# Attention in half heads: query columns in halves, row maxima 28 pairs ahead

## The chip, the cores and the metric

One Trainium2 chip, and of it one core. The metric is the time of one execution in microseconds on the device (us). The program is one launch: a mixture-of-experts layer, an attention layer, and a second mixture-of-experts layer.

## What is computed

Two sequences of 2048 tokens with 128 channels go through three residual blocks. The middle one is attention with 16 heads of 8 channels, so with both sequences there are 32 heads of 2048 queries by 2048 keys:

```python
q = _apply_rope(_rms_norm(x @ wq.T), rope_cos, rope_sin) / math.sqrt(HEAD_DIM)
k = _apply_rope(_rms_norm(x @ wk.T), rope_cos, rope_sin)
scores = jnp.einsum('bqhd,bkhd->bhqk', q, k)
attn = jax.nn.softmax(scores.astype(jnp.float32), axis=-1)
out = jnp.einsum('bhqk,bkhd->bqhd', attn, v).reshape(b, s, hidden)
return out @ wo.T
...
x = x + 0.5 * ffn(layernorm(x))
x = x + attention(layernorm(x))
x = x + 0.5 * ffn(layernorm(x))
```

The softmax needs the maximum of each query's row of scores before any exponential of that row can be taken.

## The kernel before

**Phases.** Loading, the first expert phase (`e1`), projections with rotation (`qk`), `attention_phase`, and the second expert phase (`e3`). Between phases all engines meet. What is changed lies in `attention_phase`, lines 1014 to 1326, and in the class `Late` behind it.

**Two passes over the scores.** In the first, TensorE multiplies 128 queries with 1024 keys into two banks of PSUM (`maxima`, line 1213, two matmuls of 512 columns: a *pair*), and VectorE reduces the pair to one maximum for each query (line 1301). A head has 32 pairs. The banks of two pairs alternate (`MRING = 2`), so TensorE writes a pair when VectorE has done the last but one. When all pairs of a head are reduced, VectorE takes the negative maximum (line 1315, *find*), GpSimd splits it into three bf16 parts (lines 1095 to 1101), TensorE turns them into rows (line 1226, *turn*), ScalarE copies those (line 1181), and a DMA places them beside the rows of `q_head` (line 1128). In the second pass TensorE multiplies 128 keys with 512 queries (`scores`, line 1231), and since the negative maxima are rows of the operand, the product has them subtracted. ScalarE takes the exponential out of PSUM (line 1168, *exp*). Four matmuls beside each other (`weigh`, line 1241) weigh the values with two such blocks, 1024 queries, and add up in one bank (`O`). Three banks hold scores (`SRING = 3`): the matmul for block n waits for exp n-3.

**The order.** Each engine runs a list written out by hand. I call one *step* what weighs 1024 queries with 128 keys: two score matmuls, two exps, four weighing matmuls, and, beside the scores and on other rows of the array, one pair for the maxima of a later head. A head has 32 steps. On TensorE a step is: scores, half a pair, scores, half a pair, and then the weighing of the step two before. The maxima run ahead in this way: 46 pairs stand before the first scores, and from then on (`LAG = 9`) the pairs of the head after next follow those of the next head. The turn of a head stands at its step 25 of 32, and takes one of the three score banks in its turn.

**Sums.** When a head's last step is weighed, ScalarE copies bank `O` out (`keep_sums`, line 1175), and TensorE's first weighing of the next head waits for that copy (line 1239). On ScalarE the copy stands behind the first two steps' exps of the next head. SyncE then stores the sums (line 1134) and loads `q_head` and `k_head` of the third head from there in 12 DMAs.

**Late work.** While the last steps run, and VectorE has no more maxima, the first sequence's attention output is divided, projected, added, normalized and routed (`tail_pe`, `tail_act`, `tail_dve`, numbered slots of which one stands behind each step; the highest, 37 to 40, turn the routing weights, line 1572, and VectorE copies them, line 1577). `store_comb` writes those weights to HBM, and `e3` begins by loading them from there (`e_cw`, line 733).

Of the kernel before, what the change touches and what calls it, by code (L numbers as in the profile page):

```python
# [19 lines left out]
P = 128  # L20
# [22 lines left out]
PROBS = 4  # L43
# [9 lines left out]
MR = 3  # L53
# [960 lines left out]
def attention_phase(nc, sem, kept, ps, v, identb, q, k, vals, q_rows, k_rows, qk_loaded, qk_stored,  # L1014
# [9 lines left out]
    CHUNKS = SEQ // BLK  # L1024
    STEPS = KT * CHUNKS
    PAIRS_OF_HEAD = STEPS // 2
    ENTRIES = STEPS + 1
    AHEAD, LAG = 2, 9
    TURNS = BH - AHEAD
# [4 lines left out]
    TURN_MAXIMA = LAG + 3  # L1034
    TAIL_FROM = (BH - 2) * KT + LAG + 1

    def tail(h, g, half):

        return 2 * (h * KT + g - TAIL_FROM) + half

    assert TURNS % BUFS == 0 and BUFS * ENTRIES % SRING == 0 and PAIRS_OF_HEAD % MRING == 0
# [12 lines left out]
    def turned_at(h):  # L1054

        return 0 if isinstance(h, int) and h == 0 else 1 + (h - 1) * ENTRIES + 4 * (TURN_MAXIMA + 1)

    def entry(h, g, c, last=False):

        return 1 + h * ENTRIES + g * CHUNKS + c + (1 if g > TURN_MAXIMA and not last else 0)  # L1060

    def bank(i, g, c, last=False):

        return (1 + i * ENTRIES + g * CHUNKS + c + (1 if g > TURN_MAXIMA and not last else 0)) % SRING

    def turned_bank(i):

        return (1 + (i - 1) * ENTRIES + 4 * (TURN_MAXIMA + 1)) % SRING

    with ExitStack() as tmp:  # L1070
        mx = [kept(f"mx{i}", [P, KT, 2]) for i in range(BUFS)]
        neg = [kept(f"neg{i}", [P, KT]) for i in range(BUFS)]
        res = kept("res", [P, KT])
        zero = kept("zero", [P, KT])
        mparts = [kept(f"mparts{i}", [P, MR, KT], BF16) for i in range(BUFS)]
        mrows = kept("mrows", [MR * KT, P], BF16)
# [7 lines left out]
        def _(pool):  # L1084
            def place(h, i):
                head = v[:].rearrange("p b h t d -> p (b h) t d")[:, h, :, :]
                pool.tensor_copy(vals[i][:, :, 0:HD], head).then_inc(values_placed, 1)  # L1087

            def split(h, i):

                at = h * VSTEPS
                pool.wait_ge(max_found, h + 1)
                if not (isinstance(h, int) and h < BUFS):
                    pool.wait_ge(scored, turned_at(h - BUFS) + 1)
# [8 lines left out]
            def replace(h, i):  # L1103
                pool.wait_ge(weighed, (h + 1) * KT + PRIME)
                place(h + BUFS, i)

            pool.memset(zero[:], 0.0).then_inc(max_zeroed, 1)
            for i in range(BUFS):
                place(i, i)
            pool.wait_ge(max_zeroed, 1)  # L1110
            for h in range(2 * BUFS):
                split(h, h % BUFS)
                if h:
                    replace(h - 1, (h - 1) % BUFS)
            for it in range(2, BH // BUFS - 1):
                for i in range(BUFS):
                    split(it * BUFS + i, i)
                    replace(it * BUFS + i - 1, (i - 1) % BUFS)
            for h in range((BH // BUFS - 1) * BUFS, BH):
                split(h, h % BUFS)  # L1120
                if h - 1 + BUFS < BH:
                    replace(h - 1, (h - 1) % BUFS)

        @block.sync
        def _(sp):
            def place_maxima(h, i):
                sp.wait_ge(exped, turned_at(h) + 1)
                sp.dma_start(q[i][MROW:MROW + MR, :], mrows[:]).then_inc(max_placed, 16)
# [7 lines left out]
            def turn(h, i):  # L1136
                place_maxima(h + 1, (i + 1) % BUFS)
                sp.wait_ge(weighed, (h + 1) * KT + PRIME)
                load_head(sp, q[i], k[i], q_rows[h + BUFS], k_rows[h + BUFS], qk_loaded[i])
                store_sums(h)  # L1140

            prime(sp, sums_stored)
            for h in range(1, BUFS):
                load_head(sp, q[h], k[h], q_rows[h], k_rows[h], qk_loaded[h])
            for i in range(len(qk_stored)):
                sp.wait_ge(qk_stored[i], 16 * 2 * len(range(i, NB, len(qk_stored))))
            place_maxima(0, 0)
            for it in range(0, BH // BUFS - 1):
                for i in range(BUFS):
                    turn(it * BUFS + i, i)  # L1150
            for h in range((BH // BUFS - 1) * BUFS, BH):
                if h < BH - BUFS:
                    turn(h, h % BUFS)
                else:
                    if h < BH - 1:
                        place_maxima(h + 1, (h + 1) % BUFS)
                    store_sums(h)
                if h == BH - 3:
                    late.load_sums(sp, 0)
                if h == BH - 2:  # L1160
                    late.store_comb(sp, 0)

        @block.scalar
        def _(act):
            def exps(h, i, g, last=False):
                for c in range(CHUNKS):
                    act.wait_ge(scored, entry(h, g, c, last) + 1)
                    act.activation(prob[:, g % PROBS, c, :], ps[:, S + bank(i, g, c, last), :], ACT.Exp).then_inc(exped, 1)  # L1168
                    if c % 2:
                        late.tail_act(act, tail(h, g, c // 2), M)  # L1170

            def keep_sums(h):
                act.wait_ge(weighed, (h + 1) * KT + PRIME)
# [3 lines left out]
            def keep_maxima(h, bank_at):  # L1177
                act.wait_ge(scored, turned_at(h) + 1)
                if not (isinstance(h, int) and h == 0):
                    act.wait_ge(max_placed, 16 * h)  # L1180
                act.activation(mrows[:], ps[0:MR * KT, S + bank_at, 0:P], ACT.Copy).then_inc(exped, 1)

            def turn(h, i, last=False):
                for g in range(1, KT):
                    if not (isinstance(h, int) and h == 0 and g < PROBS):

                        act.wait_ge(weighed, h * KT + max(g - PROBS, -1) + 1 + PRIME)
                    exps(h, i, g, last)
                    if g == TURN_MAXIMA and not last:
                        keep_maxima(h + 1, turned_bank(i + 1))  # L1190
# [6 lines left out]
            keep_maxima(0, 0)  # L1197
            exps(0, 0, 0)
            for it in range(0, TURNS // BUFS):
                for i in range(BUFS):  # L1200
                    turn(it * BUFS + i, i)
            turn(BH - 2, (BH - 2) % BUFS)
            turn(BH - 1, (BH - 1) % BUFS, last=True)

        @block.tensor
        def _(pe):
            def maxima(h, i, j):

                n, c = h * PAIRS_OF_HEAD + j // 2, j % CHUNKS
                if j % 2 == 0 and not (isinstance(n, int) and n < MRING):  # L1210
                    pe.wait_ge(max_reduced, n - MRING + 1)
                at = M + 2 * (j // 2 % MRING) + j % 2
                one = pe.matmul(ps[:, at, :], q[i][HALF:HALF + KR, (j // CHUNKS) * P:(j // CHUNKS + 1) * P],  # L1213
                                k[i][HALF:HALF + KR, c * BLK:(c + 1) * BLK], start=True, stop=True)
                if j % 2:
                    one.then_inc(max_scored, 1)

            def free(n):

                if not (isinstance(n, int) and n < SRING):  # L1220
                    pe.wait_ge(exped, n - SRING + 1)

            def turn_maxima(h, i, bank_at):
                free(turned_at(h))
                pe.wait_ge(max_split, (h + 1) * VSTEPS)
                pe.matmul(ps[0:MR * KT, S + bank_at, 0:P], mparts[i][:].rearrange("p a t -> p (a t)"), identb[:],
                          start=True, stop=True).then_inc(scored, 1)

            def scores(h, i, g, c, last=False):
                free(entry(h, g, c, last))  # L1230
                pe.matmul(ps[:, S + bank(i, g, c, last), :], k[i][0:KS, g * P:(g + 1) * P],  # L1231
                          q[i][0:KS, c * BLK:(c + 1) * BLK], start=True, stop=True).then_inc(scored, 1)

            def weigh(h, i, g, half, last=False):

                pe.wait_ge(exped, entry(h, g, 2 * half + 1, last) + 1)
# [3 lines left out]
                for j in range(4):  # L1240
                    done_one = pe.matmul(ps[32 * j:32 * j + 32, O, half * HALF_BLK:(half + 1) * HALF_BLK], vals[i][:, g, :],  # L1241
# [621 lines left out]
```

## Time and profile before

| | |
|---|---|
| median of 3 runs | 1897.98 us |
| lowest and highest | 1893.78 and 1899.74 us |
| span of the profiled execution | 1896.1 us |
| instructions in it | 37685 |
| TensorE busy | 1781.2 us, 94% |
| VectorE busy | 1620.7 us, 85% |
| ScalarE busy | 1459.6 us, 77% |
| GpSimd busy | 344.2 us, 18% |
| attention phase, first maxima to the first load of `e3` | 386.54 to 1638.65 us |

The profiler's span runs from the first to the last instruction. It is the profiled execution's own time as far as the page has one, and it stands 1.9 us below the median of the runs. PE is TensorE, DVE VectorE, ACT ScalarE, POOL GpSimd, SP SyncE, and PEld is TensorE's load of weights. The ends of matmuls are modelled and overlap, so a busy PE can still have time to give; the distance from the start of a matmul to the start of the same matmul one step later says more. An instruction's row names what ended the idle time before it.

### The profile page before, as it was taken

To read this page: it belongs to the slowest core of one execution; us is meant where nothing else is said; L and a number is where in the kernel's file an instruction comes from. 1 tells how busy PE (TensorE), PEld (TensorE's weight loads), DVE (VectorE), ACT (ScalarE), POOL (GpSimd) and SP (SyncE) were. 2 spreads that over 40 slices of the span, in tenths; PEclk is the share of its full clock that TensorE was granted. 3 is DMA by queue.
4 is the path that set the end of the run, shared out by engine and by line. 5 is a ranking of instruction groups with operands and counts; after the bars stand their busy time and mean duration, and the time that the engine had idled before them with its cause. 6 is when DMAs were issued, how large, how long until landed. Compare 5 with 4: busy or idle time off the path is not lost. (4 is left out here: it accounts for less than half of the span.)

```text
span 1896.1 us, 37685 instructions
## 1 busy us (share of the span) xinstructions
PE 1781.2 (94%) x14923; PEld 750.2 (40%) x14923; DVE 1620.7 (85%) x1950; ACT 1459.6 (77%) x2715; POOL 344.2 (18%) x416
## 2 busy tenths in 40 slices
PE   5699998879999999999999999999999999899998
PEld 3488776702222222222222222222222223377786
DVE  6466775689999999999999999999999993386765
ACT  2356564606999999999999999999999996546455
POOL 4266551300000000000000000000000000145565
PEclk9799997857999999999999999999999998999999
DMA  4453330220010010000001001000000010444463
GB/s 117 88 128 127 103 110 1 93 91 2 25 33 20 20 36 22 20 31 27 20 25 33 20 20 37 21 20 31 26 20 26 33 28 3 85 109 109 102 144 78
DMA packets 66309, 98.81 MB, mean 52 GB/s; under 512 B 11995, under 2 KB 33312, under 8 KB 66116
## 3 DMA queue, kind: packets, MB, share of 16 engines
q1 hardware_dynamic: 61974, 94.32, 18.4%
q10 hardware_dynamic: 4160, 2.10, 0.4%
q8 instruction: 117, 1.92, 0.4%
q14 instruction: 58, 0.48, 0.1%
HBM read 84.94 MB, written 11.04 MB: 51 GB/s over the span
## 5 line engine op out<-in xcount | busy, mean ns | idle before, releaser
L1301 DVE TENSOR_REDUCE at_mx<-ps 128x1 f32<-128x1024 f32 x1024 | 1166.1, 1216 | 9.8 <-PE ps L1213 7.7
L1168 ACT ACTIVATE at_prob<-ps 128x512 f32<-128x512 f32 x2048 | 1098.2, 596 | 77.0 <-PE ps L1231 31.8
L1241 PE MATMUL ps<-at_prob,vals 128*32 128x256 f32 x8192 | 656.9, 392 | 13.3 <-ACT at_sums L1175 13.3
L1213 PE MATMUL ps<-k_head,q_head 48*128 48x512 bf16 x2048 | 638.8, 392 | 14.3 <-PEq L800 7.5
L1231 PE MATMUL ps<-q_head,k_head 51*128 51x512 bf16 x1924 | 584.5, 383 | 2.8 <-ACT at_prob L1168 2.8
L1241 PEld LDWEIGHTS ps<-at_prob,vals 128*32 128x32 f32 x8192 | 162.4, 108 | 429.5 <-ACT at_prob L1168 409.0
L688 POOL TENSOR_TENSOR e_part<-e_silu,e_cw 128x512 f32<-128x512 f32 (+1 forms) x208 | 268.1, 1289 | 311.5 <-ACT e_silu L659 124.3
L700 DVE TENSOR_TENSOR ps<-e_part,ps 128x512 f32<-128x512 f32 (+1 forms) x208 | 144.5, 695 | 157.6 <-POOL e_part L688 157.1
L1231 PEld LDWEIGHTS ps<-q_head,k_head 51*128 51x128 bf16 x1924 | 117.5, 93 | 404.1 <-ACT at_prob L1168 385.3
L659 ACT ACTIVATE e_silu<-ps 128x512 f32<-128x512 f32 (+1 forms) x208 | 124.2, 597 | 143.8 <-PE ps L615 141.9
L1095 POOL TENSOR_TENSOR at_mparts<-at_neg,at_zero 128x16 bf16<-128x16 f32 x32 | 7.0, 220 | 796.5 <-DVE at_neg L1315 796.5
L1213 PEld LDWEIGHTS ps<-k_head,q_head 48*128 48x128 bf16 x2048 | 119.8, 94 | 55.2 <-DVE at_mx L1301 44.8
L666 ACT ACTIVATE q_head<-ps 128x512 fp32r<-128x512 f32 (+1 forms) x156 | 93.1, 597 | 44.8 <-DVE ps L700 34.2
L615 PE MATMUL ps<-xnT_hi,wgate_hi 128*128 128x512 f32 x208 | 88.6, 426 | 20.0 <-ACT e_silu L659 13.7
L706 DVE TENSOR_TENSOR q_head<-ps,q_head 128x512 fp32r<-128x512 f32 (+1 forms) x156 | 106.6, 684 | 0.4
L633 PE MATMUL ps<-q_head,wdown_hi 128*128 128x512 f32 (+1 forms) x312 | 98.1, 395 | 2.4 <-DVE q_head L706 2.4
L615 PE MATMUL ps<-xnT_lo,wgate_hi 128*128 128x512 f32 x208 | 82.6, 397 | 0.0
L615 PE MATMUL ps<-xnT_hi,wgate_lo 128*128 128x512 f32 x208 | 82.2, 395 | 0.0
L623 PE MATMUL ps<-xnT_hi,wup_hi 128*128 128x512 f32 x192 | 76.1, 396 | 0.0
L623 PE MATMUL ps<-xnT_lo,wup_hi 128*128 128x512 f32 x192 | 75.9, 395 | 0.0
L623 PE MATMUL ps<-xnT_hi,wup_lo 128*128 128x512 f32 x192 | 75.8, 395 | 0.0
L1087 POOL COPY vals<-v 128x128 f32<-128x128 f32 x32 | 9.1, 290 | 332.6 <-PE ps L1241 332.6
(258 smaller groups left out, 1294.2 us busy)
## 6 DMA issues: line engine op xcount, KB each, us to landing
e_cw<-comb_rows SPq DMA_DIRECT2D x80, 256.0 KB, 3.3
e_cw<-comb_rows SPq DMA_DIRECT2D x32, 224.0 KB, 3.1
e_cw<-comb_rows SPq DMA_DIRECT2D x32, 192.0 KB, 3.3
q_head<-q_rows SPq DMA_DIRECT2D x64, 96.0 KB
k_head<-k_rows SPq DMA_DIRECT2D x64, 96.0 KB
e_cw<-comb_rows SPq DMA_DIRECT2D x32, 160.0 KB, 2.9
e_cw<-comb_rows SPq DMA_DIRECT2D x48, 96.0 KB, 2.8
e_cw<-comb_rows SPq DMA_DIRECT2D x32, 128.0 KB, 3.1
```

Of the source, the lines that this page charges most:

```text
L615: last = pe.matmul(ps[:, gate_bank(n), :], wgate[wp][:, cols], xnT[xp][:, tokens], start=(m == 0), stop=(m == len(PASSES) - 1))
L623: last = pe.matmul(ps[:, UP + n % UPS, :], wup[wp][:, cols], xnT[xp][:, tokens], start=(m == 0), stop=(m == len(PASSES) - 1))
L633: last = pe.matmul(ps[:, Y, :], wdown[wp][0:rows[c], c, :], hidden[hp][n % HIDDENS][0:rows[c], :], start=(c == 0 and m == 0), stop=(c == C ...
L659: act.activation(silu[0:r, n % 2, :], ps[0:r, gate_bank(n), :], ACT.Silu).then_inc(silued, 1)
L688: pool.tensor_tensor(part[0:r, n % 2, :], silu[0:r, n % 2, :], cw[0:r, n % CW, :], ALU.mult).then_inc(weighted, 1)
L700: dve.tensor_tensor(ps[0:rows[c], UP + n % UPS, :], part[0:rows[c], n % 2, :], up, ALU.mult).then_inc(product, 1)
L706: dve.tensor_tensor(hidden[LO][n % HIDDENS][0:r, :], ps[0:r, UP + n % UPS, :], hidden[HI][n % HIDDENS][0:r, :].bitcast(F32), ALU.subtract) ...
L1168: act.activation(prob[:, g % PROBS, c, :], ps[:, S + bank(i, g, c, last), :], ACT.Exp).then_inc(exped, 1)
L1213: one = pe.matmul(ps[:, at, :], q[i][HALF:HALF + KR, (j // CHUNKS) * P:(j // CHUNKS + 1) * P], k[i][HALF:HALF + KR, c * BLK:(c + 1) * BLK] ...
L1231: pe.matmul(ps[:, S + bank(i, g, c, last), :], k[i][0:KS, g * P:(g + 1) * P], q[i][0:KS, c * BLK:(c + 1) * BLK], start=True, stop=True).th ...
L1241: done_one = pe.matmul(ps[32 * j:32 * j + 32, O, half * HALF_BLK:(half + 1) * HALF_BLK], vals[i][:, g, :], prob[:, g % PROBS, 2 * half + j ...
L1301: dve.tensor_reduce(mx[i][:, j // 2, j % 2:j % 2 + 1], ps[:, at:at + 2, :].rearrange("p a t -> p (a t)"), AX.X, ALU.max).then_inc(max_redu ...
```

## The change

A *unit* is now half a head: 16 key tiles by 1024 queries, 16 steps and 16 pairs. There are 64 units. The maxima of a unit cover only its 1024 queries, and find, split, turn, copy and placing DMA are done for each unit, on half the columns: 64 times instead of 32. The pairs run `LEAD = 28` steps ahead of the scores, all along, so 28 pairs stand before the first scores. A step is what it was: the same two score matmuls, two exps, a pair, and the weighing of the step two before (`WEIGH_AFTER = 2`). The exps of the two halves of a key tile, which were neighbours, are now 16 steps apart, and the probabilities have 8 slots of one step instead of 4 slots of two, in the same memory.

Around that, four things move. The turn stands behind step 9 of each unit, and behind the step's weighing instead of ahead of its second half. `keep_sums` stands behind the exps of step 2 of the next head. SyncE's order in a head becomes: store sums, place maxima, load, place maxima; and at the end `store_comb` stands behind the last store of sums. The late work begins at step 997 of 1024, where it began at step 980, and its slots from 29 on (of 41) stand behind the attention's last step.

The core of the diff:

```diff
-PROBS = 4
+PROBS = 8
...
-    PAIRS_OF_HEAD = STEPS // 2
-    ENTRIES = STEPS + 1
-    AHEAD, LAG = 2, 9
-    TURNS = BH - AHEAD
+    UNITS = 2 * BH
+    CHUNKS = 2
+    TILES = SEQ // P // 2
+    PAIRS_OF_UNIT = 2 * TILES
+    STEPS = UNITS * KT
+    ENTRIES = KT * CHUNKS + 1
+    LEAD = PAIRS_OF_UNIT + 12
+    TURN = 9
+    WEIGH_AFTER = 2
...
-    TURN_MAXIMA = LAG + 3
-    TAIL_FROM = (BH - 2) * KT + LAG + 1
...
+    TAIL_FROM = STEPS - LEAD + 1
...
         @block.sync
...
+            for h in range(BH):
+                if h >= 1:
+                    store_sums(h - 1)
+                place_maxima(2 * h + 1)
+                if h >= 1 and h - 1 + BUFS < BH:
+                    sp.wait_ge(weighed, head_done(h - 1))
+                    load(h - 1 + BUFS)
+                if h < BH - 1:
+                    place_maxima(2 * h + 2)
                 if h == BH - 2:
-                    late.store_comb(sp, 0)
+                    late.load_sums(sp, 0)
+            store_sums(BH - 1)
+            late.store_comb(sp, 0)
...
         @block.scalar
...
+            def exps(t):
+                if t >= PROBS:
+                    act.wait_ge(weighed, t - PROBS + 1 + PRIME)
                 for c in range(CHUNKS):
...
-                if not last:
-                    act.wait_ge(weighed, (h + 1) * KT - PROBS + 1 + PRIME)
-                    exps(h + 1, i + 1, 0)
-                keep_sums(h)
...
+            for t in range(STEPS):
+                u, g = divmod(t, KT)
+                exps(t)
+                if g == TURN and u < UNITS - 1:
+                    keep_maxima(u + 1)
+                late.tail_act(act, t - TAIL_FROM, M)
+                if t >= 2 * KT and t % (2 * KT) == WEIGH_AFTER:
+                    keep_sums(t // (2 * KT) - 1)
+            keep_sums(BH - 1)
+            for t in range(STEPS, TAIL_FROM + late.TAIL):
+                late.tail_act(act, t - TAIL_FROM, M)
...
         @block.tensor
...
+            for r in range(LEAD):
+                for one in range(2):
+                    maxima(r, one)
+                if r == PAIRS_OF_UNIT + 4:
+                    turn_maxima(0)
+            for t in range(STEPS + WEIGH_AFTER):
+                u, g = divmod(t, KT)
+                for c in range(CHUNKS):
+                    if t < STEPS:
+                        scores(t, c)
+                    if t + LEAD < STEPS:
+                        maxima(t + LEAD, c)
+                if t >= WEIGH_AFTER:
+                    weigh(t - WEIGH_AFTER)
+                if g == TURN and u < UNITS - 1:
+                    turn_maxima(u + 1)
+                late.tail_pe(pe, t - TAIL_FROM, M)
...
         @block.vector
...
+            for r in range(STEPS):
+                reduce(r)
+                if r >= PAIRS_OF_UNIT and r % PAIRS_OF_UNIT == 1:
+                    find(r // PAIRS_OF_UNIT - 1)
+            find(UNITS - 1)
```

Ahead of the first scores on TensorE (the names: `k_head` by `q_head` is a matmul for maxima, `identb` a turn, `q_head` by `k_head` scores) stood, before:

```order
L1213 MATMUL ps<-k_head0,q_head0 128x512 x64
L1213 MATMUL ps<-k_head1,q_head1 128x512 x13
L1226 MATMUL ps<-identb,at_mparts0 48x128
L1213 MATMUL ps<-k_head1,q_head1 128x512 x15
L1231 MATMUL ps<-q_head0,k_head0 128x512 x5
```

and now:

```order
L1194 MATMUL ps<-k_head0,q_head0 128x512 x42
L1208 MATMUL ps<-identb,at_mparts0 24x128
L1194 MATMUL ps<-k_head0,q_head0 128x512 x14
L1218 MATMUL ps<-q_head0,k_head0 128x512
L1194 MATMUL ps<-k_head0,q_head0 128x512
L1218 MATMUL ps<-q_head0,k_head0 128x512
```

The 92 matmuls for maxima before the first scores have become 56, and all of them are of the first head.

On ScalarE, from the first exps to the third head (`at_prob` is an exp, `at_mrows` the copy of turned maxima, `at_sums` the copy of the sums), stood, before:

```order
L1168 ACTIVATE at_prob<-ps 128x512 x52
L1181 ACTIVATE at_mrows<-ps 48x128
L1168 ACTIVATE at_prob<-ps 128x512 x16
L1175 ACTIVATE at_sums<-ps 128x512
L1168 ACTIVATE at_prob<-ps 128x512 x48
L1181 ACTIVATE at_mrows<-ps 48x128
L1168 ACTIVATE at_prob<-ps 128x512 x16
L1175 ACTIVATE at_sums<-ps 128x512
```

and now:

```order
L1155 ACTIVATE at_prob<-ps 128x512 x20
L1167 ACTIVATE at_mrows<-ps 24x128
L1155 ACTIVATE at_prob<-ps 128x512 x32
L1167 ACTIVATE at_mrows<-ps 24x128
L1155 ACTIVATE at_prob<-ps 128x512 x18
L1160 ACTIVATE at_sums<-ps 128x512
L1155 ACTIVATE at_prob<-ps 128x512 x14
L1167 ACTIVATE at_mrows<-ps 24x128
L1155 ACTIVATE at_prob<-ps 128x512 x32
```

A head has 64 exps. The first copy of sums stood behind 68 of them, 4 of the next head, and stands behind 70, 6 of the next head; the copies of maxima stand twice in a head.

At the end of the phase SyncE had, behind its loads of the late work (`at_o`), before:

```order
L1128 DMA q_head<-at_mrows 3x16x128
L1134 DMA sum_rows<-at_sums 18x1x256 x4
L1582 DMA comb_rows<-v 9x2048
L1134 DMA sum_rows<-at_sums 18x1x256 x4
L1070 UNCONDITIONAL_BRANCH
```

and now:

```order
L1121 DMA sum_rows<-at_sums 18x1x256 x4
L1115 DMA q_head<-at_mrows 3x8x128
L1121 DMA sum_rows<-at_sums 18x1x256 x4
L1536 DMA comb_rows<-v 9x2048
L1066 UNCONDITIONAL_BRANCH
```

The store of the routing weights (`comb_rows`) has moved behind the last sums and is the last DMA of the phase.

## Rows read from the trace of the kernel before

**Rows 1.** The page: engines' busy us; a group's busy us, mean ns.

```profile
PE 1781.2 (94%) x14923; PEld 750.2 (40%) x14923; DVE 1620.7 (85%) x1950; ACT 1459.6 (77%) x2715; POOL 344.2 (18%) x416
...
L1301 DVE TENSOR_REDUCE at_mx<-ps 128x1 f32<-128x1024 f32 x1024 | 1166.1, 1216 | 9.8 <-PE ps L1213 7.7
```

**Rows 2.** Stretches: us, then busy time of PE, PEld, DVE, ACT, POOL, and PEclk.

```profile
386.00:440.00 54.00, 46.56 (x93) 6.36 (x95) 52.02 (x46) 1.55 (x2) 1.68 (x8) 0.50 0.11 41
439.79:446.38 6.59, 6.30 (x32) 1.25 (x34) 4.73 (x4) 4.13 (x8) 0.00 (x0) 0.50 0.01 4
478.00:1535.00 1057.00, 1044.61 (x11167) 269.00 (x11165) 1054.98 (x958) 1009.83 (x1915) 33.78 (x145) 1.00 0.08 26
1589.84:1603.49 13.65, 13.65 (x67) 5.03 (x59) 4.12 (x11) 6.55 (x13) 0.00 (x0) 0.50 0.00 1
```

**Rows 3.** Instructions in order: start, us, engine; first maxima, first scores.

```profile
386.54 1.86 PE L1213 MATMUL ps<-k_head,q_head 48*128 48x512 bf16 x4 [7.45 <-PEq L800]
...
439.79 0.60 PE L1231 MATMUL ps<-q_head,k_head 51*128 51x512 bf16 x1
```

**Rows 4.** Instructions in order: steps in the middle of a head.

```profile
999.36 6.87 DVE L1301 TENSOR_REDUCE at_mx<-ps 128x1 f32<-128x1024 f32 x6
...
1000.74 0.39 PE L1231 MATMUL ps<-q_head,k_head 51*128 51x512 bf16 x1
...
1001.28 0.64 PE L1241 MATMUL ps<-at_prob,vals 128*32 128x256 f32 x8
...
1004.60 0.64 PE L1241 MATMUL ps<-at_prob,vals 128*32 128x256 f32 x8
```

**Rows 5.** Instructions in order: the boundary between two heads; the next copy of sums.

```profile
989.60 1.08 ACT L1168 ACTIVATE at_prob<-ps 128x512 f32<-128x512 f32 x2
989.71 0.64 PE L1241 MATMUL ps<-at_prob,vals 128*32 128x256 f32 x8
...
990.57 0.60 ACT L1175 ACTIVATE at_sums<-ps 128x512 f32<-128x512 f32 x1
...
991.32 0.64 PE L1241 MATMUL ps<-at_prob,vals 128*32 128x256 f32 x8 [0.43 <-ACT at_sums L1175]
...
1027.02 0.60 ACT L1175 ACTIVATE at_sums<-ps 128x512 f32<-128x512 f32 x1
```

**Rows 6.** Instructions in order: a turn on PE, and ACT behind it.

```profile
1017.09 0.24 PE L1226 MATMUL ps<-identb,at_mparts 128*48 128x128 bf16 x1
1017.26 0.64 PE L1241 MATMUL ps<-at_prob,vals 128*32 128x256 f32 x8
1017.83 0.39 PE L1231 MATMUL ps<-q_head,k_head 51*128 51x512 bf16 x1
...
1018.32 1.09 ACT L1168 ACTIVATE at_prob<-ps 128x512 f32<-128x512 f32 x2
```

**Rows 7.** The tile of the sums: ns min/median/max of one, first and last start.

```profile
L1175 ACT ACTIVATE at_sums<-ps x32: 597/605/605, 480.2 to 1634.1; 128x512 f32<-128x512 f32 x32
```

**Rows 8.** Instructions in order: from the last maxima to the first load of `e3`.

```profile
1557.62 0.60 PE L1231 MATMUL ps<-q_head,k_head 51*128 51x512 bf16 x2
...
1589.16 0.39 PE L1231 MATMUL ps<-q_head,k_head 51*128 51x512 bf16 x1 [2.47 <-ACT at_prob L1168]
...
1622.27 0.26 DVE L1565 RECIPROCAL at_comb<-at_ex 128x16 f32<-128x16 f32 x1
...
1629.70 0.68 DVE L1577 COPY v<-ps 9x512 f32<-9x512 f32 x1 [0.96 <-PE ps L1572]
...
1638.65 2.22 SPq L733 DMA_DIRECT2D e_cw<-comb_rows  x5
```

**Rows 9.** The chain that ended last: start, us; the same store for the second sequence.

```profile
1775.80 2.41 DMA comb_rows<-v
```

**Rows 10.** Instructions in order: two steps at the lower clock, first head.

```profile
444.07 0.60 PE L1231 MATMUL ps<-q_head,k_head 51*128 51x512 bf16 x1
...
446.05 0.53 PE L1231 MATMUL ps<-q_head,k_head 51*128 51x512 bf16 x1
```

More of the change, by code:

```diff
@@ L1142, in _ @@
             prime(sp, sums_stored)
             for h in range(1, BUFS):
-                load_head(sp, q[h], k[h], q_rows[h], k_rows[h], qk_loaded[h])
+                load(h)
             for i in range(len(qk_stored)):
                 sp.wait_ge(qk_stored[i], 16 * 2 * len(range(i, NB, len(qk_stored))))
[L1147 to L1158, printed above, removed]
+            place_maxima(0)
@@ L1196, in _, with keep_maxima @@
-            prime(act, sums_kept)
[L1197 to L1203, printed above, removed]
+            def keep_maxima(u):
+                n = turned_at(u)
+                act.wait_ge(scored, n + 1)
+                if u:
+                    act.wait_ge(max_placed, 16 * u)
+                act.activation(mrows[:], ps[0:MR * TILES, S + n % SRING, 0:P], ACT.Copy).then_inc(exped, 1)
@@ L1205, in _, with maxima @@
         @block.tensor
         def _(pe):
[L1207 to L1216, printed above, removed]
+            def maxima(r, one):
+                u, j = divmod(r, PAIRS_OF_UNIT)
+                h, half = divmod(u, 2)
+                if one == 0 and r % (2 * PAIRS_OF_UNIT) == 0:
+                    pe.wait_ge(qk_loaded[h % BUFS], 16 * LOAD_DMAS * (h // BUFS + 1))
+                if one == 0 and r >= MRING:
+                    pe.wait_ge(max_reduced, r - MRING + 1)
+                tile, c = half * TILES + j // 2, 2 * (j % 2) + one
+                made = pe.matmul(ps[:, M + 2 * (r % MRING) + one, :], q[h % BUFS][HALF:HALF + KR, tile * P:(tile + 1) * P],
+                                 k[h % BUFS][HALF:HALF + KR, c * BLK:(c + 1) * BLK], start=True, stop=True)
+                if one:
+                    made.then_inc(max_scored, 1)
@@ L1218, in free @@
             def free(n):
-                if not (isinstance(n, int) and n < SRING):
+                if n >= SRING:
                     pe.wait_ge(exped, n - SRING + 1)
[L1223 to L1226, printed above, removed]
-                          start=True, stop=True).then_inc(scored, 1)
[L1229 to L1232, printed above, removed]
@@ L1234, in weigh, with turn_maxima, scores @@
-            def weigh(h, i, g, half, last=False):
-                pe.wait_ge(exped, entry(h, g, 2 * half + 1, last) + 1)
+            def turn_maxima(u):
+                n = turned_at(u)
+                free(n)
+                pe.wait_ge(max_split, (u + 1) * VSTEPS)
+                pe.matmul(ps[0:MR * TILES, S + n % SRING, 0:P], mparts[u % BUFS][:].rearrange("p a t -> p (a t)"), identb[:],
+                          start=True, stop=True).then_inc(scored, 1)
+            def scores(t, c):
+                u, g = divmod(t, KT)
+                h, half = divmod(u, 2)
+                n, at = entry(t, c), (2 * half + c) * BLK
+                if g == 0 and c == 0:
+                    pe.wait_ge(max_placed, 16 * (u + 1))
+                free(n)
+                pe.matmul(ps[:, S + n % SRING, :], k[h % BUFS][0:KS, g * P:(g + 1) * P],
+                          q[h % BUFS][0:KS, at:at + BLK], start=True, stop=True).then_inc(scored, 1)
@@ L1273, in pe_next @@
-            def pe_next(h, nxt, c, i):
-                free(entry(h + 1, 0, c))
-                pe.matmul(ps[:, S + bank(i + 1, 0, c), :], k[nxt][0:KS, 0:P],
-                          q[nxt][0:KS, c * BLK:(c + 1) * BLK], start=True, stop=True).then_inc(scored, 1)
-            prime(pe, weighed)
-            for h in range(AHEAD):
-                pe.wait_ge(qk_loaded[h], 16 * LOAD_DMAS)
-                for j in range(STEPS if h == 0 else (KT - LAG) * CHUNKS):
-                    maxima(h, h, j)
-                    if h == 1 and j == 3 * CHUNKS:
-                        turn_maxima(0, 0, 0)
```

192 lines of the change are left out of this document (65 added, 127 removed).

## The prediction, made before the changed kernel ran

> **What bounds the kernel now.** I read the page's busy times first, then stretches, then single steps. Over the whole span TensorE is 94% busy and VectorE 85% [rows 1], which is a mean over stages; attention alone takes 1252 us of the 1896 [rows 3, 8], and there the stretch of 29 heads says more: of 1057 us VectorE is busy 1054.98, TensorE 1044.61, ScalarE 1009.83 [rows 2]. Three engines are close together, so I take each engine's own pace. VectorE: six reductions in a row take 6.87 us [rows 4]; less the last one's own 1.216 [rows 1], five distances are 5.65, so 1.131 a pair. TensorE, where it waits for nobody: from one weighing to the third after it 3.32 us, so 1.107 a step [rows 4]. A head is 36.45 us from one copy of sums to the next [rows 5]. VectorE's 32 pairs are 36.2 of that, and the find fills most of the rest. VectorE sets the pace, and TensorE has 32 x 1.107 = 35.4 of its own, plus what interrupts it: 0.5 at the boundary, where the first weighing of a head stands 1.61 us behind the last of the one before instead of 1.107, released by the copy of sums [rows 5], and some 0.2 at a turn [rows 6]. So TensorE needs 36.1 of 36.45. It is 0.3 us a head from being the bound, and that margin is what I watch in this change.
>
> **The change part by part.**
>
> *Fewer pairs ahead.* Before the first scores VectorE is the one that is busy (52.02 of 54 us), at TensorE's lower clock [rows 2], and the first scores start with the 46th pair: 439.79 - 386.54 = 53.25 us for 45 pairs, 1.183 each [rows 3]. Now they start with the 28th: 27 x 1.183 = 31.9. **Gain 21.3 us.** The unit's turn stands 7 pairs ahead of that, 8 us, for a copy and a small DMA; before it had 7 as well.
>
> *A step.* The matmuls, exps and pairs of a step are the same in number and size, and so is the distance from exp to weighing. Each pair of exps now has a second wait (slots of one step); before every other one had it. The wait is long satisfied, and from the start of a pair of exps to what follows on ScalarE are 0.97 us [rows 5], so 0.13 a step lies free under TensorE's 1.107. I take nothing; only what a second wait costs beyond 0.13 would add to each of 1024 steps.
>
> *The boundary.* This is the large term. `keep_sums` stands behind the exps of the third step of a head, not the second, while TensorE's first weighing still stands directly behind the third step's scores and waits for that copy. Counted from the start of the third step's first score: ScalarE's pair of exps starts 0.49 us after it (1017.83 to 1018.32) [rows 6]; the copy of sums follows 0.97 after the pair's start, and the weighing is released 0.75 after the copy's start (989.60, 990.57, 991.32) [rows 5]. So the weighing starts at 2.21, where it would start at 0.54 (1000.74 to 1001.28) [rows 4]. TensorE waits **1.67 us at each boundary instead of 0.50**. Behind the waiting weighing stand, in TensorE's order, the next step's scores and maxima, so VectorE, which has one pair ready, runs dry too, about 1.4 us. Bounds: no less than 0.5 if the copy got in between the exps, which its place in the list excludes; no more than 1.8, if the second wait uses up those 0.13.
>
> *The turn.* Twice a head, for half the columns. The matmul delays what stands behind it 0.17 us (1017.09 to 1017.26) [rows 6]. The turn takes one score bank, so the second score of the next step waits for an exp that ends about 1.58 us after the turning step's start (0.49, a distance of 0.49, and 0.60) while it would start at 1.51; with its release that is 0.12 more. So 0.29 each, bounds 0.17 and 0.40. The chain ahead of it (find, four short GpSimd operations) has two pairs' time, 2.26 us, and the DMA behind it has 6 steps, as before; I take nothing for either. The second find adds less than 0.1 us on VectorE, which is no longer the bound.
>
> *Loads and stores.* On SyncE 12 loads now stand between the two placings of a head, 13 steps ahead of the second; at 0.44 an issue (five in 2.22) [rows 8] that is 5 us, at twice as much 11. The loaded head is wanted 25 steps later, 28 us. I take nothing.
>
> *The attention loop, summed.* From the first score to the first step without maxima TensorE has 997 steps: 997 x 1.107 = 1103.7. Boundaries in it: 31 x 1.67 = 51.8. Turns: 62 x 0.29 = 18.0. The start at the lower clock: the first copy of sums is at 480.2 [rows 7], 40.4 us after the first score, where 33 steps, a turn and 1.46 to the copy make 38.2; the start costs 2.2, now as before. Sum 1175.7. VectorE's need in the same loop is 997 x 1.131 + 62 x 0.09 = 1133, so TensorE is the bound by a wide margin: 37.7 us a head. Before, the loop was 1557.62 - 439.79 = 1117.8 [rows 3, 8] for 980 steps. **Loss 57.9 us**, of which 19 are the 17 more steps with maxima that the shorter lead shifts here.
>
> *The late work.* Before, `e3`'s first load was issued 81.0 us after the first step without maxima (1557.62 to 1638.65), with attention's own end and its stores in between; the routing weights were ready at 64.9 (1622.27 and 0.26) and copied by 72.8 (1629.70 and 0.68) [rows 8]. VectorE's chain up to the weights I leave at 64.9: its slots up to 28 still lie beside attention steps. Then the four turns and copies stand alone: between 4 x 0.68 + 0.6 = 3.3 and, with TensorE at the lower clock after waiting, 5; I take 4.7. The store is now on the path: 2.4 [rows 9] and its issue 0.3. So 72.3 or 72.5 instead of 81.0. **Gain 8.5 us**, bounds 5 and 11. `e3` itself is untouched.
>
> Sum against the profiled span: 1896.1 - 21.3 + 57.9 - 8.5 = 1924.2. The median of the runs is 1.9 above the span, so **1926 us**. The bounds of the boundary, turn and late work give 1915 to 1938.
>
> **The rivals.**
>
> *The clock falls too.* In the late work TensorE stood idle 2.47 us [rows 8], and right behind that its granted clock was 0.50, the 1.2 GHz level, for 13.65 us; in the 29 heads, with 0.43 us of idling at each boundary, it stayed at 1.00 [rows 2, 5]. The new idling at each boundary is 1.6 us, between the two. A step at the lower clock is 1.98 us [rows 10] for 1.107. At the start the clock came back 6.6 us after the first scores [rows 2]; a fall as long costs 6.6 x (1 - 1.107/1.98) = 2.9 us. At half of the boundaries that is 45 us: 1971; at a few of them, 1935 to 1950. For it: the idling comes at every head. Against: two thirds of the row's 2.47 us, with dense work on both sides. By the Trainium skill ("TensorE: Matmul & The Clock Gate", section "HAM oscillation — how this bites in real kernels") a wait that recurs in every turn of a loop can throttle the clock anew in every turn; no run here shows that yet, and the 0.50 behind the 2.47 us agrees that one wait can do it. Chance 0.13.
>
> *The boundary is hidden, no change.* If the weighing waited 0.5 us as before (the copy not really behind those exps, or TensorE's later matmuls passing it), TensorE's need is 35.4 + 0.5 + 0.6 = 36.5 and VectorE's 36.4: 36.6 a head, 31 x 1.1 = 34 us less than forecast, 1892 to 1900. Against it: in the rows the engines keep their written order [rows 5]. Chance 0.11.
>
> *Faster.* If TensorE's interruptions overlap with VectorE's backlog so that heads stay at 36.45, the loop is 997/980 of before, plus 19, and the sum is 1896.1 - 21.3 + 19 - 8.5 + 1.9 = 1887. It decides at a TensorE need of 36.4 a head; I find 37.7. Chance 0.06.
>
> **How the numbers follow.** Forecast 0.70, clock 0.13, no change 0.11, faster 0.06. About 0.3% (6 us) can be told from no change: faster 0.07, same 0.12, slower 0.81. The forecast's own range is 1915 to 1938; it reaches on to part of the clock's case and a little way towards no change: 1908 to 1952.
>
> **What would show it.** Right: first scores 31.9 us after the first maxima; a row of weighing at each of 31 boundaries with the copy of sums as its releaser and some 1.6 us of idling (about 50 us in all); copies of sums 37.7 us apart; VectorE idle over 1 us a head; granted clock 1.00 in the heads; `e3`'s first load about 72 us after the last maxima. Wrong: copies 36.5 apart (no or little stall), a granted clock under 1.00 in the middle stretch (the clock), turns that wait for the split, or late work that takes 80 us as before.

## The result, and the profile after

The changed kernel takes **1936.45 us** (median of four runs, 1934.51 to 1952.33), the kernel before 1896.57 (1893.78 to 1899.74): a ratio of 1.0231, 95% interval 1.0193 to 1.0270. The profiled execution's span is 1933.9 us against 1896.1, so 37.8 us more.

The page's busy times of the changed kernel, and three of its costliest groups (busy us, mean ns of one, then idle time of the engine just before and what ended it; L1265 reduces, L1230 weighs, L1155 are the exps), which answer to [rows 1]:

```profile
PE 1775.8 (92%) x14955; PEld 752.7 (39%) x14955; DVE 1625.4 (84%) x1982; ACT 1476.6 (76%) x2747; POOL 365.3 (19%) x544
...
L1265 DVE TENSOR_REDUCE at_mx<-ps 128x1 f32<-128x1024 f32 x1024 | 1170.9, 1216 | 57.3 <-PE ps L1194 56.9
L1155 ACT ACTIVATE at_prob<-ps 128x512 f32<-128x512 f32 x2048 | 1110.2, 595 | 115.2 <-PE ps L1218 94.4
L1230 PE MATMUL ps<-at_prob,vals 128*32 128x256 f32 x8192 | 663.5, 396 | 49.5 <-ACT at_sums L1160 49.5
```

A reduction lasts 1216 ns as before. What is new is waiting: VectorE idles 57.3 us ahead of its reductions, where it was 9.8 [rows 1], and TensorE 49.5 us ahead of weighings, all of it ended by the copy of sums.

Stretches of the changed kernel (us, then busy time of PE, PEld, DVE, ACT, POOL, PEclk, DMA share, GB/s): the maxima alone, the start of the loop, some 30 heads, and one stretch inside these.

```profile
379.50:411.56 32.06, 27.81 (x56) 3.74 (x56) 30.68 (x28) 1.55 (x2) 1.61 (x8) 0.50 0.19 68
411.56:417.70 6.14, 5.71 (x26) 0.94 (x26) 5.82 (x5) 3.36 (x6) 0.00 (x0) 0.50 0.00 0
454.00:1591.00 1137.00, 1084.65 (x11484) 281.91 (x11484) 1087.34 (x1013) 1050.68 (x1995) 54.64 (x269) 0.99 0.07 24
494.35:497.76 3.41, 3.41 (x24) 0.47 (x16) 2.40 (x2) 1.96 (x5) 0.00 (x0) 0.50 0.11 22
```

In the long stretch no engine is full any more: VectorE, full within 2 us of 1057 before [rows 2], is idle 50 us of 1137. And the granted clock, 1.00 in the heads before, is 0.99, with stretches at 0.50.

The boundary in order (start, us, engine, line; in brackets the engine's idle time and what ended it), first one at which the clock fell, then the next, at which it didn't, with the copy after it:

```profile
492.30 0.61 ACT L1160 ACTIVATE at_sums<-ps 128x512 f32<-128x512 f32 x1
...
493.05 0.64 PE L1230 MATMUL ps<-at_prob,vals 128*32 128x256 f32 x8 [1.60 <-ACT at_sums L1160]
...
494.30 1.22 DVE L1265 TENSOR_REDUCE at_mx<-ps 128x1 f32<-128x1024 f32 x1 [1.30 <-PE ps L1194]
495.04 0.60 PE L1218 MATMUL ps<-q_head,k_head 51*128 51x512 bf16 x1
...
497.02 0.60 PE L1218 MATMUL ps<-q_head,k_head 51*128 51x512 bf16 x1
...
529.60 0.64 PE L1230 MATMUL ps<-at_prob,vals 128*32 128x256 f32 x8
...
531.62 0.61 ACT L1160 ACTIVATE at_sums<-ps 128x512 f32<-128x512 f32 x1
...
532.38 0.64 PE L1230 MATMUL ps<-at_prob,vals 128*32 128x256 f32 x8 [1.60 <-ACT at_sums L1160]
...
569.42 0.60 ACT L1160 ACTIVATE at_sums<-ps 128x512 f32<-128x512 f32 x1
```

The weighing that stood 1.61 us behind the last one [rows 5] stands 532.38 - 529.60 = 2.78 behind it, so it waits 2.78 - 1.107 = 1.67 us. From copy to copy it is 37.80 us (531.62 to 569.42), before 36.45 [rows 5]. After the first of the two boundaries it is 39.32 (492.30 to 531.62): there one step (495.04 to 497.02) takes the 1.98 us of the lower clock [rows 10]. Of the 31 boundaries 8 are like that one, and 23 like the second.

A turn in order, ahead of the next weighing; then the find of the same head's second unit (L1273) between weighings, with the second turn ahead of the last of them; then the late work, from the first step without maxima to the first load of `e3`:

```profile
960.60 0.64 PE L1230 MATMUL ps<-at_prob,vals 128*32 128x256 f32 x8
961.06 0.22 PE L1208 MATMUL ps<-identb,at_mparts 128*24 128x128 bf16 x1
...
962.01 0.64 PE L1230 MATMUL ps<-at_prob,vals 128*32 128x256 f32 x8
...
975.29 0.64 PE L1230 MATMUL ps<-at_prob,vals 128*32 128x256 f32 x8
...
975.74 0.16 DVE L1273 TENSOR_REDUCE at_neg<-at_mx 128x8 f32<-128x16 f32 x1
...
978.75 0.64 PE L1230 MATMUL ps<-at_prob,vals 128*32 128x256 f32 x8
...
980.13 0.64 PE L1230 MATMUL ps<-at_prob,vals 128*32 128x256 f32 x8
...
1603.33 0.60 PE L1218 MATMUL ps<-q_head,k_head 51*128 51x512 bf16 x2
...
1668.80 0.26 DVE L1519 RECIPROCAL at_comb<-at_ex 128x16 f32<-128x16 f32 x1
1669.11 3.28 PE L1526 MATMUL ps<-ident,at_comb 128*9 128x128 f32 x16 [8.36 <-DVE at_comb L1519]
...
1671.88 1.28 DVE L1531 COPY v<-ps 9x512 f32<-9x512 f32 x2 [0.18 <-PE ps L1526]
1673.18 0.29 SPq L1536 DMA_DIRECT2D comb_rows<-v  x1
...
1675.62 0.37 SPq L733 DMA_DIRECT2D e_cw<-comb_rows  x1
```

The difference of the two profiled spans, by stretches: the phases ahead of attention -6.7 (first maxima at 379.83, before at 386.54 [rows 3]; in nine profiled executions of all kernels here it lies between 378.6 and 386.5, so the change isn't in it), maxima ahead of the first scores -21.5 (31.73 instead of 53.25), the loop +73.9 (411.56 to 1603.33, 1191.8 instead of 1117.8), the late work -8.7 (72.3 instead of 81.0), the rest +0.8. Sum 37.8.

### The profile page after: what moved, and what is told of

It is laid out like the page before. It is cut to its first block, busy times and chain, and to the rows that moved or that the text cites. A ratio compares the mean times of both kernels' runs of the same rounds, so it can differ in the third digit from the quotient of the medians.

```text
span 1933.9 us, 38702 instructions
## 1 busy us (share of the span) xinstructions
PE 1775.8 (92%) x14955; PEld 752.7 (39%) x14955; DVE 1625.4 (84%) x1982; ACT 1476.6 (76%) x2747; POOL 365.3 (19%) x544
## 4 chain that ended last, share of the span: by engine, by line
PE 44%; ACT 27%; issue 4%; DVE 3%; DMA 1%; POOL 1%; SPq 0%; POOLq 0%; ACTq 0%; DVEq 0%
ACT at_prob L1155 26%; PE ps L1230 17%; PE ps L1218 16%; PE ps L615 3%; PE ps L633 3%; PE ps L623 3%; DVE at_mx L1265 2%; ACT at_sums L1160 1%; POOL e_part L688 1%; DMA e_cw<-comb_rows 1%; PE ps L1194 1%; PE ps L1349 0%; PE ps L1364 0%; DVE ps L700 0%; PE ps L1434 0%
## 5 line engine op out<-in xcount | busy, mean ns | idle before, releaser
L1265 DVE TENSOR_REDUCE at_mx<-ps 128x1 f32<-128x1024 f32 x1024 | 1170.9, 1216 | 57.3 <-PE ps L1194 56.9
L1155 ACT ACTIVATE at_prob<-ps 128x512 f32<-128x512 f32 x2048 | 1110.2, 595 | 115.2 <-PE ps L1218 94.4
L1230 PE MATMUL ps<-at_prob,vals 128*32 128x256 f32 x8192 | 663.5, 396 | 49.5 <-ACT at_sums L1160 49.5
L1194 PE MATMUL ps<-k_head,q_head 48*128 48x512 bf16 x2048 | 647.5, 392 | 12.1 <-PEq L800 7.7
L1218 PE MATMUL ps<-q_head,k_head 51*128 51x512 bf16 x2048 | 638.4, 387 | 7.4 <-ACT at_prob L1155 2.5
L1230 PEld LDWEIGHTS ps<-at_prob,vals 128*32 128x32 f32 x8192 | 162.9, 108 | 470.7 <-ACT at_prob L1155 423.9
L1218 PEld LDWEIGHTS ps<-q_head,k_head 51*128 51x128 bf16 x2048 | 130.2, 93 | 444.4 <-ACT at_prob L1155 398.5
L1091 POOL TENSOR_TENSOR at_mparts<-at_neg,at_zero 128x8 bf16<-128x8 f32 x64 | 12.8, 200 | 1152.1 <-DVE at_neg L1273 1152.1
L1194 PEld LDWEIGHTS ps<-k_head,q_head 48*128 48x128 bf16 x2048 | 127.5, 93 | 38.6 <-DVE at_mx L1265 29.5
L633 PEld LDWEIGHTS ps<-q_head,wdown_hi 128*128 128x128 f32 (+1 forms) x312 | 57.6, 188 | 19.7 <-issue 4.2
```

Of the source, the lines that this page charges most:

```text
L633: last = pe.matmul(ps[:, Y, :], wdown[wp][0:rows[c], c, :], hidden[hp][n % HIDDENS][0:rows[c], :], start=(c == 0 and m == 0), stop=(c == C ...
L1155: act.activation(prob[:, t % PROBS, c, :], ps[:, S + n % SRING, :], ACT.Exp).then_inc(exped, 1)
L1194: made = pe.matmul(ps[:, M + 2 * (r % MRING) + one, :], q[h % BUFS][HALF:HALF + KR, tile * P:(tile + 1) * P], k[h % BUFS][HALF:HALF + KR, ...
L1218: pe.matmul(ps[:, S + n % SRING, :], k[h % BUFS][0:KS, g * P:(g + 1) * P], q[h % BUFS][0:KS, at:at + BLK], start=True, stop=True).then_inc ...
L1265: dve.tensor_reduce(mx[u % BUFS][:, j // 2, j % 2:j % 2 + 1], ps[:, at:at + 2, :].rearrange("p a t -> p (a t)"), AX.X, ALU.max).then_inc(m ...
```

## The experiments

**The copy of sums back in its place.** One line of the changed kernel is undone:

```diff
-                if t >= 2 * KT and t % (2 * KT) == WEIGH_AFTER:
+                if t >= 2 * KT and t % (2 * KT) == WEIGH_AFTER - 1:
                     keep_sums(t // (2 * KT) - 1)
```

> The changed kernel with one thing undone: ScalarE copies a head's sums behind the exponentials of the next head's second step, as before, and not behind those of the third. My theory, that the place of this copy is what the boundary costs: the first weighing of a head waits some 0.5 us instead of 1.67, copies of sums are 36.4 to 36.7 us apart instead of 37.8, the granted clock stays at 1.00 in the heads, and the time is 1884 to 1893 us. Rival, that units of half a head cost their time elsewhere (twice as many turns, a second wait in each pair of exponentials) and the wait only shows it: copies stay 37.5 us apart or more, and the time is 1925 or more.

Measured: **1889.32 us** (ten runs, 1883.97 to 1894.94), 0.9974 of before, interval 0.9955 to 0.9994. Its group of weighings on the page:

```profile
L1230 PE MATMUL ps<-at_prob,vals 128*32 128x256 f32 x8192 | 657.0, 392 | 15.2 <-ACT at_sums L1160 15.2
```

Two copies of sums that follow each other, in order:

```profile
973.59 0.61 ACT L1160 ACTIVATE at_sums<-ps 128x512 f32<-128x512 f32 x1
...
1010.28 0.60 ACT L1160 ACTIVATE at_sums<-ps 128x512 f32<-128x512 f32 x1
```

The stretch of its heads (columns as above):

```profile
460.00:1560.00 1100.00, 1080.53 (x11574) 283.38 (x11576) 1094.05 (x1020) 1055.47 (x2009) 54.66 (x269) 1.00 0.08 26
```

The wait is 0.49 us a boundary (15.2 / 31), a head takes 36.69, the clock stays at 1.00, VectorE is full again. One line, two exps further on in ScalarE's list, carries the whole loss of 47 us; the half heads without it are no slower than before.

**That line alone in the kernel before.** `keep_sums` moves behind the first two exps of the next head's second group; nothing else is changed.

```diff
                     if c % 2:
                         late.tail_act(act, tail(h, g, c // 2), M)
+                    if c == 1 and g == 1 and h > 0:
+                        keep_sums(h - 1)
...
                     exps(h + 1, i + 1, 0)
-                keep_sums(h)
+                else:
+                    keep_sums(h)
```

> The kernel before with one part of the change alone: the copy of a head's sums moves two exponentials later, behind the first two of the next head's second group of four, as in the changed kernel; nothing of the half heads. My theory: TensorE's need of 36.1 us a head grows by 1.2 at the boundary to 37.3, above VectorE's 36.4, so heads are about 37.3 us apart, and at some boundaries the granted clock falls to 0.5; 30 x 0.85 = 26 us more, up to 38 with falls: 1920 to 1936. Rival (the half heads themselves cost the time): heads stay at 36.5, and the time is 1895 to 1902.

Measured: 1965.37 us (1960.96 to 1974.33), 1.0382, interval 1.0342 to 1.0422: more than expected. Its group of weighings on the page:

```profile
L1244 PE MATMUL ps<-at_prob,vals 128*32 128x256 f32 x8192 | 672.0, 400 | 49.7 <-ACT at_sums L1177 49.7
```

Two copies of sums in order:

```profile
597.23 0.60 ACT L1177 ACTIVATE at_sums<-ps 128x512 f32<-128x512 f32 x1
...
634.85 0.60 ACT L1177 ACTIVATE at_sums<-ps 128x512 f32<-128x512 f32 x1
```

The stretch of its heads, and one of its late work:

```profile
484.00:1568.00 1084.00, 1039.10 (x11004) 265.16 (x10996) 1039.22 (x941) 996.85 (x1883) 32.62 (x140) 0.99 0.08 25
1631.49:1696.34 64.85, 64.12 (x306) 17.50 (x304) 14.90 (x46) 34.24 (x67) 0.00 (x0) 0.50 0.01 2
```

The wait is the same 49.7 us, without any half heads. A head takes 37.62 (expected 37.3, rival 36.5): it grows by the whole 1.17 us by which the wait is longer, and the slack that the expectation counted on takes up none of it. The clock falls at six places in the loop, and the loop is 47.5 us longer. Another 21.4 us lie in the late work (102.4 instead of 81.0), which neither theory had: there TensorE stays at the lower clock for 64.85 us, where it was 13.65 in its first such stretch before [rows 2]. Of the expectation the direction holds; a head is 0.3 us longer than expected, and the total lies above the range.

**The first weighing behind the next step.** With the sums copied early, TensorE passes over the first weighing of a head and does it, and the second, behind the next step's scores and maxima.

```diff
-                if t >= WEIGH_AFTER:
+                first = t >= 2 * KT and t % (2 * KT) == WEIGH_AFTER
+                if t >= WEIGH_AFTER and not first:
+                    if t >= 2 * KT and t % (2 * KT) == WEIGH_AFTER + 1:
+                        weigh(t - WEIGH_AFTER - 1)
                     weigh(t - WEIGH_AFTER)
```

> The changed kernel with the sums copied behind the second step's exponentials, and the first weighing of a head put one step later, ahead of the second weighing, so that TensorE has the fourth step's scores and maxima to do while the sums are copied. My theory: TensorE waits nowhere at the boundary, its need is 32 x 1.107 + 2 x 0.35 = 36.1 us a head, VectorE's is 32 x 1.131 + 2 x 0.1 = 36.4 and is the bound again; copies of sums 36.4 us apart, no falls of the clock, 1878 to 1887 us. Rival, that after the copy is moved back nothing is left to gain at the boundary: the same as the kernel with the copy moved back, within 2 us.

Measured: 1897.8 us (ten runs, 1890.43 to 1900.42), 1.0009, interval 0.9983 to 1.0034. My theory fell: TensorE waits for no copy any more, yet a head takes 36.73. Its boundary in order:

```profile
966.81 0.39 PE L1218 MATMUL ps<-q_head,k_head 51*128 51x512 bf16 x1
...
967.37 0.39 PE L1194 MATMUL ps<-k_head,q_head 48*128 48x512 bf16 x1 [0.18 <-DVE at_mx L1268]
...
968.11 1.07 PE L1230 MATMUL ps<-at_prob,vals 128*32 128x256 f32 x16
...
969.86 2.36 DVE L1268 TENSOR_REDUCE at_mx<-ps 128x1 f32<-128x1024 f32 x2 [0.28 <-PE ps L1194]
```

And a stretch of its late work:

```profile
1589.01:1640.21 51.20, 41.28 (x179) 18.28 (x180) 14.31 (x41) 18.00 (x37) 0.43 (x1) 0.50 0.07 14
```

TensorE gets to the next step early, but the half pair there has to wait for VectorE (0.18 us; only two pairs have room), and so runs 0.56 behind the score that it otherwise runs beside. The time saved on one wait is spent on another, and VectorE still loses 0.28. The 8.5 us to the first experiment lie mostly behind the loop (late work of 78.8 us instead of 71.5), where the clock stays at 0.50 for 51.2 us; what keeps it there is not settled.

**The first weighing between the halves of the next step.**

```diff
                     if t + LEAD < STEPS:
                         maxima(t + LEAD, c)
+                    if c == 0 and t >= 2 * KT and t % (2 * KT) == WEIGH_AFTER + 1:
+                        weigh(t - WEIGH_AFTER - 1)
-                if t >= WEIGH_AFTER:
+                if t >= WEIGH_AFTER and not (t >= 2 * KT and t % (2 * KT) == WEIGH_AFTER):
                     weigh(t - WEIGH_AFTER)
```

> The kernel with the sums copied early (the first experiment), and the first weighing of a head moved behind the first score and the first half pair of maxima of the next step, where in the third experiment it stood behind that whole step and doubled up with the second weighing. My theory: there VectorE lost 0.36 us because two weighings in a row held back its next pair; here the pair comes 0.43 us sooner, TensorE has some 0.45 us of work while it waits for the copy, and VectorE sets the pace with 32 x 1.131 + 2 x 0.08 = 36.35: copies of sums 36.35 to 36.5 us apart instead of 36.69, 1878 to 1885 us. Rival, that VectorE loses the same anywhere since the whole delay of a boundary is more than its backlog of one pair: 36.7 us a head and 1889 as in the first experiment.

Measured: 1895.56 us (twelve runs, 1892.89 to 1903.66), 1.0017, interval 1.0002 to 1.0032; a head takes 36.77, close to the rival's 36.7, though the time is 6 us above the rival's 1889. The boundary in order:

```profile
972.05 0.39 PE L1218 MATMUL ps<-q_head,k_head 51*128 51x512 bf16 x1
...
972.61 0.39 PE L1194 MATMUL ps<-k_head,q_head 48*128 48x512 bf16 x1 [0.17 <-DVE at_mx L1267]
972.93 0.64 PE L1230 MATMUL ps<-at_prob,vals 128*32 128x256 f32 x8
...
973.96 3.53 DVE L1267 TENSOR_REDUCE at_mx<-ps 128x1 f32<-128x1024 f32 x3 [0.27 <-PE ps L1194]
```

The same wait for VectorE stands in front of the weighing, and VectorE loses the same 0.27 us. With room for two pairs the last half us of the boundary can't be hidden by reordering TensorE in these two ways.

**A longer wait.** In the changed kernel ScalarE copies the sums once more, into a spare buffer, ahead of the real copy:

```diff
+                act.activation(spare[:], ps[:, O, :], ACT.Copy)
                 act.activation(sums[:], ps[:, O, :], ACT.Copy).then_inc(sums_kept, 1)
```

> The changed kernel with the sums copied once more ahead of the real copy (into a spare buffer), which makes the wait of the first weighing longer and nothing else. Both theories: TensorE's idling at a boundary grows from 1.60 us by 0.5 to 0.6 to some 2.2, a head from 37.8 to 38.4, 31 x 0.6 = 18 us more. If how long TensorE idles decides whether the clock falls: falls at most boundaries (20 or more of 31, against 8), 1.5 us each, so 18 or more beyond that, 1972 us or more. If it is the place of the idling in some period, whatever its length: again some 8 falls, and 1950 to 1960.

Measured: 1980.2 us (1968.01 to 1991.82), 1.0454, interval 1.0397 to 1.0511. The group of weighings on the page:

```profile
L1232 PE MATMUL ps<-at_prob,vals 128*32 128x256 f32 x8192 | 673.1, 401 | 65.0 <-ACT at_sums L1162 65.0
```

Two copies of sums, without a fall between them:

```profile
534.33 0.62 ACT L1162 ACTIVATE at_sums<-ps 128x512 f32<-128x512 f32 x1
...
572.61 0.62 ACT L1162 ACTIVATE at_sums<-ps 128x512 f32<-128x512 f32 x1
```

The stretch of the heads, and one of the longest at the lower clock:

```profile
457.00:1600.00 1143.00, 1077.56 (x11218) 276.07 (x11218) 1063.74 (x987) 1039.53 (x1974) 53.56 (x261) 0.97 0.08 24
810.11:820.35 10.24, 9.70 (x60) 1.70 (x60) 4.98 (x6) 4.80 (x10) 0.81 (x4) 0.50 0.04 9
```

TensorE idles 2.10 us a boundary (65.0 / 31), a head without a fall takes 38.28, so the wait itself adds 31 x 0.48 = 15 us. The loop is 34.7 us longer, so the falls account for 20 more. There are 16 of them instead of 8, some of them longer, and the clock over the heads is 0.97 instead of 0.99. The count is that of the profiled execution, at 1968.01 us the fastest of the four; how many falls the others had is not on record. It is between the expected 20 or more and 8: how long TensorE idles matters, and it is not all that matters.

**The same wait, filled.** The changed kernel, with five score matmuls, whose results are overwritten, ahead of the wait for the copy:

```diff
+                    if h:
+                        n = entry(t + WEIGH_AFTER + 1, 0)
+                        free(n)
+                        for _ in range(5):
+                            pe.matmul(ps[:, S + n % SRING, :], k[h % BUFS][0:KS, 0:P], q[h % BUFS][0:KS, 0:BLK], start=True, stop=True)
                     pe.wait_ge(sums_kept, h + PRIME)
```

> The changed kernel, with the wait of each first weighing left as it is, but TensorE kept at work for most of it: five score matmuls of the step that comes next but one are issued ahead of the wait for the copied sums, each overwritten later by the real one (they are extra work, and nothing uses them). 5 x 0.22 = 1.1 us, so the wait left over is some 0.5 us instead of 1.60. If the falls of the clock come from TensorE's idling: heads stay 37.8 us apart, none of the 31 boundaries is longer, and the time is 12 us less than the changed kernel's, 1920 to 1926. If they come from the wait's place in the program or from elsewhere: again some 8 heads of 39.3 us, and 1934 to 1940. If the five matmuls themselves hold up VectorE: heads over 37.9.

Measured: **1922.33 us** (1917.19 to 1924.94), 1.0146, interval 1.0126 to 1.0166. A boundary and two later copies of sums, in order:

```profile
494.92 1.24 PE L1232 MATMUL ps<-q_head,k_head 51*128 51x512 bf16 x5
495.76 0.61 ACT L1160 ACTIVATE at_sums<-ps 128x512 f32<-128x512 f32 x1
...
496.42 0.64 PE L1235 MATMUL ps<-at_prob,vals 128*32 128x256 f32 x8 [0.27 <-ACT at_sums L1160]
...
533.47 0.60 ACT L1160 ACTIVATE at_sums<-ps 128x512 f32<-128x512 f32 x1
...
571.17 0.60 ACT L1160 ACTIVATE at_sums<-ps 128x512 f32<-128x512 f32 x1
```

The stretch of the heads:

```profile
459.00:1588.00 1129.00, 1116.47 (x11721) 293.86 (x11713) 1092.89 (x1019) 1057.59 (x2007) 54.64 (x269) 1.00 0.08 25
```

A head takes 37.70, no boundary is longer, the clock is 1.00, and the time is in the range expected for this case. So the falls come from TensorE's idling. The kernel gains 14 us, of which 3 are another thing (the weighing starts 0.66 us behind the copy's start instead of 0.75, 31 times 0.1); the other 11 are about what the falls cost.

**Three pairs more ahead.** With the sums copied early:

```diff
-    LEAD = PAIRS_OF_UNIT + 12
+    LEAD = PAIRS_OF_UNIT + 15
```

> The kernel with the sums copied early, and the maxima running 31 pairs ahead instead of 28, to price a pair of lead by itself. My theory, by the prediction's own working: a pair that runs ahead costs 1.18 us before the first scores and takes a step of 1.147 (36.69 / 32) out of the loop, so nearly nothing: first maxima to first scores 35.3 instead of 31.7, the loop 3.4 us shorter, 1888 to 1892 us. Rival, that fewer pairs ahead is a gain by itself: the loop stays, and 3 more pairs cost 3.5 us, 1893.

Measured: 1893.16 us (ten runs, 1887.39 to 1903.97), 0.9996, interval 0.9979 to 1.0014, which is not told apart from the first experiment's. In the traces the first scores stand 35.25 us behind the first maxima instead of 31.74, and the loop is 1141.4 us instead of 1145.3. What three more pairs cost ahead of the loop, 3.5, they give back in it, 3.9: a pair of lead costs next to nothing here. It is the rows that say so; the two times expected, 1888 to 1892 and 1893, are too close to be told apart.

## Why the prediction was right, and where its sum was off

The direction and its reason hold; the time lies 10.4 us above the forecast, inside the range. (The bounds that the prediction names for boundary, turn and late work add up to 1916 to 1940, not 1915 to 1938; nothing hangs on that.)

- *Fewer pairs ahead*: 21.3 forecast, 21.5 measured. That most of it comes back as steps with maxima in the loop was part of the sum, and the last experiment shows it by itself.
- *The boundary*: 1.67 forecast, 2.78 - 1.107 = 1.67 measured, at each of 31 places, with the copy of sums as its releaser, and VectorE dry for 1.30. The first two experiments show the cause from both sides: without the moved copy it is gone, and the moved copy alone brings it into the kernel before. That the boundary would hide (the rival of no change) is out.
- *The turn*: 0.29 forecast for each. The first of a head takes 962.01 - 960.60 - 1.107 = 0.30, the second 980.13 - 978.75 - 1.107 = 0.27. But the find, which I took at nothing since VectorE would no longer be the bound, holds up TensorE's next pairs in the second unit by 0.13 us a head, 4 us in all (the three steps from 975.29 to 978.75 take 3.46 us instead of 3.32). Cover was assumed where VectorE was still just behind.
- *A head*: 37.7 forecast, 37.80 measured: 32 x 1.107 + 1.67 + 0.30 + 0.27 + 0.13. The second wait in each pair of exps costs nothing that shows.
- *The late work*: 72.5 forecast, 72.3 measured. The weights are ready at 65.7 (forecast 64.9) and copied 4.1 later (4.7), and the store with its issue takes 2.44 (2.7).
- *The clock*: this step failed. I held that it would stay at 1.00, since 1.6 us of idling is two thirds of the 2.47 us behind which it had fallen, and I named a clock under 1.00 in the middle stretch as a sign of being wrong. It fell at 8 of 31 boundaries, by 1.5 us each (39.32 - 37.80), 12.1 us in all. The rival of the clock was therefore in part the truth, with its price too high: I took 6.6 us at the lower clock for each fall, where it was 3.41, and 3.41 x (1 - 1.107/1.98) = 1.5. The rule cited there from the Trainium skill ("TensorE: Matmul & The Clock Gate", section "HAM oscillation — how this bites in real kernels") is that a wait which recurs in each turn of a loop can throttle the clock anew in each. The 8 falls agree with it; the 23 boundaries without a fall show that the same wait does not do so each time.
- *The sum*: falls +12.1, finds +4.0, the start of the loop +0.9, one step counted too many -1.1, rest of the loop +0.2, ahead of the loop and the late work -0.4, the phases before and behind attention -5.9, median over span 2.55 instead of 1.9, +0.65. Together 10.4. The -5.9 is chance of the profiled execution as far as the traces tell, and it covered half of what the falls cost: without it the forecast would have been 16 us off. That the number lies so near is in part luck.

Open: why these 8 boundaries. They look regular in time: the falls stand at 494.35, 685.49, 723.04 and 801.55 us, and 611 us later (16 heads) again, at 1105.33, 1296.48, 1334.03 and 1412.53. With the longer wait (the copy done twice) there is such an order too: the falls at 1014.91, 1093.42, 1209.47, 1287.98 and 1404.03 us are each followed by another after 194.56 (five heads). Since each boundary of the changed kernel idles the same 1.60 us, when it comes seems to decide. That is not shown: no run here moved a boundary in time alone.

## What to carry to other kernels

A copy that another engine waits for costs what is queued ahead of it on its own engine: count, at each such wait, the instructions between the event that allows the copy and the copy, before and after a reordering; here two exps more in one list were worth 47 us. Shortening the lead here only moved work from ahead of the loop into it, and gained next to nothing by itself; look for idle time in the loop that it could fill. And a wait on TensorE had two prices here, its length and what the clock did: work that nobody needs took the second away where the first had to stay.

## What was not expected of the hardware

- Equal waits, unequal clock: of 31 boundaries, each with 1.60 us of idling, 8 brought the clock to 0.50 and 23 did not; with 2.10 us it was 16 falls, with 0.49 none (one profiled execution of each kernel), and none with 1.67 us of waiting of which all but 0.27 was filled.
- At the end of attention, where each step has less work for TensorE, the clock stayed at 0.50 for very different times in kernels with nearly the same work there: 64.85 us in the second experiment and 51.20 in the third, 13.65 at first in the kernel before [rows 2]. Where it was longest the late work took 21.4 us more than before; such a difference hides gains of a few us in the loop. Why it differs is open.
- A weighing starts 0.75 us behind the start of the copy that releases it, whether TensorE has idled 0.43 us [rows 5] or 1.60. Only behind the filled wait, with 0.27 us of idling left, it starts 0.66 behind. Why is open.
